# Output products placed between the q projection and the turn of the decayed keys, in a one-core attention and mixture-of-experts kernel

## The reference, cut to what matters

```
xn = _layernorm(x, axis=-1)
q, k, v = silu(xn Wq), silu(xn Wk), silu(xn Wv)           # 16 heads of 32
o = lightning_attn(q, k, v, log_decay)                    # chunks of 128 tokens
gate = (xn Wg1) Wg2
o = o * sigmoid(gate); o = o * rsqrt(mean(o*o over a head) + eps) * norm_w
x = x + o Wo + ffn(xn)                                    # ffn: top 2 of 8 experts, w1, relu, w2
```

## Time and profile before

| what | value |
|---|---|
| median of 3 runs | 2012.76 us (2012.4 to 2012.93) |
| profiled execution | 2013.65 us, of it 2011.9 us span |
| TensorE busy | 1992.8 us, 99% of the span |
| VectorE busy | 892.4 us, 44% |
| ScalarE busy | 552.1 us, 27% |
| GpSimd busy | 721.1 us, 36% |
| mean granted TensorE clock | 0.998 |

### The profile page before, as it was taken

One profiled execution on the slowest core, in us unless ns is written; L12 is line 12 of the kernel. 1 busy time (PEld: TensorE's weight loads), 2 busy tenths in 40 slices (PEclk: granted clock), 3 DMA queues, 4 the chain that ended last, 5 costly groups with the idle time before them and its releaser, 6 DMA issues.

```text
span 2011.9 us, 29144 instructions
## 1 busy us (share of the span) xinstructions
PE 1992.8 (99%) x11768; PEld 1651.0 (82%) x11768; DVE 892.4 (44%) x1792; ACT 552.1 (27%) x986; POOL 721.1 (36%) x600
## 2 busy tenths in 40 slices
PE   8999999999999999999999999999999999999998
PEld 7888888888788888888888888888888888888886
DVE  7777677776742234235323432422252234224311
ACT  6322232223332123124123312421242123123211
POOL 4555553555341323314332331422142324233211
PEclk9999999999999999999999999999999999999999
DMA  6112112211442133315323331521152125224121
GB/s 209 60 64 86 48 61 79 71 66 56 135 135 30 51 79 117 49 48 142 59 63 80 110 50 46 150 50 33 47 160 36 40 47 159 36 62 108 34 33 21
DMA packets 85506, 151.46 MB, mean 75 GB/s; under 512 B 18304, under 2 KB 18304, under 8 KB 85360
## 3 DMA queue, kind: packets, MB, share of 16 engines
q1 hardware_dynamic: 61312, 105.64, 16.4%
q0 software_dynamic: 24048, 43.76, 12.8%
HBM read 109.82 MB, written 39.53 MB: 74 GB/s over the span
## 4 chain that ended last, share of the span: by engine, by line
PE 94%; DMA 2%; issue 1%; DVE 1%; POOL 1%; ACT 0%; POOLq 0%; SPq 0%; DVEq 0%; ACTq 0%
PE bank L1269 47%; PE bank L1562 34%; PE bank L1402 4%; PE bank L1323 2%; PE bank L1617 2%; DMA raw_weights<-in_L_ffn_w 2%; PE bank L1391 1%; PE bank L1276 1%; PE bank L1385 1%; PE bank L1297 1%; PE bank L1358 1%; PE bank L1368 0%; POOL head_scale L588 0%; DMA attn_raw<-in_L_attn_Wv 0%; DMA x_in<-in_L_attn_x 0%
## 5 line engine op out<-in xcount | busy, mean ns | idle before, releaser
L1216 DVE SCALAR_TENSOR_TENSOR h_lo<-bank,h_hi 128x512 fp32r<-128x512 f32 x254 | 175.2, 690 | 745.8 <-ACT h_hi L849 745.6
L632 POOL DMA_INDIRECT gathered<-xn_rows,gather_row x304 | 320.1, 1053 | 476.7 <-DVE x_blocks L1069 294.7
L1269 PE MATMUL bank<-xT_hi,w_hi 128*128 128x512 f32 x1024 | 398.9, 390 | 0.3
L1269 PE MATMUL bank<-xT_lo,w_hi 128*128 128x512 f32 x1024 | 398.5, 389 | 0.0
L1269 PE MATMUL bank<-xT_hi,w_lo 128*128 128x512 f32 x1024 | 398.5, 389 | 0.0
L1562 PE MATMUL bank<-w_hi,h_hi 128*128 128x512 f32 x1016 | 395.5, 389 | 0.7 <-DVE h_lo L1216 0.7
L1562 PE MATMUL bank<-w_hi,h_lo 128*128 128x512 f32 x1016 | 395.3, 389 | 0.0
L1562 PE MATMUL bank<-w_lo,h_hi 128*128 128x512 f32 x1016 | 395.3, 389 | 0.0
L849 ACT ACTIVATE h_hi<-bank 128x512 fp32r<-128x512 f32 x254 | 151.7, 597 | 797.5 <-PE bank L1269 797.5
L645 POOL DMA_INDIRECT out_rows<-y,add_row x80 | 128.8, 1610 | 546.2 <-ACT y L842 473.0
L1269 PEld LDWEIGHTS bank<-xT_hi,w_hi 128*128 128x128 f32 x1024 | 192.2, 188 | 41.7 <-issue 1.7
(11 more groups left out here) (217 smaller groups left out, 2300.1 us busy)
## 6 DMA issues: line engine op xcount, KB each, us to landing
raw_weights<-in_L_ffn_w SPq DMA_DIRECT2D x256, 256.0 KB, 11.7
x_in<-in_L_attn_x SPq DMA_DIRECT2D x32, 256.0 KB, 3.6
xn_rows<-xn SPq DMA_DIRECT2D x32, 256.0 KB, 2.8
x_res<-in_L_attn_x SPq DMA_DIRECT2D x32, 256.0 KB, 5.0
out_rows<-y_attn SPq DMA_DIRECT2D x28, 256.0 KB, 2.0
gathered<-xn_rows,gather_row POOLq DMA_INDIRECT x304
out_rows<-y,add_row POOLq DMA_INDIRECT x80, 5.1
attn_raw<-in_L_attn_Wq SPq DMA_DIRECT2D x4, 256.0 KB, 4.9
```

The lines of the kernel that those rows point to most:

```text
L632: pool.indirect_dma_start(xg[:, nth % 2, q * P:(q + 1) * P], None, xn_pieces, bass.IndirectOffsetOnAxis(ap=gather_row[:, col, q:q + 1], ax ...
L1216: v_.scalar_tensor_tensor(lo[:, 0:n * P], h_bank[f % 2][:, 0:n * P], 0.0, hi[:, 0:n * P].bitcast(F32), ALU.max, ALU.subtract).then_inc(S[" ...
L1269: last = mm(dest, at(left[l], t), at_r(right[r], t), start=(i == 0), stop=(i == n - 1))
```

## The change

Nothing is computed otherwise. In the second slot of groups 1 to 7:

- TensorE makes the four output products behind the q projection, ahead of `turn_kd(u + 1)`, `attend(u)` and `update_states(u + 1)`, and no longer behind these.
- The banks of the output products are swapped: tiles 0 and 2 go to `proj[1]`, tiles 1 and 3 to `proj[0]`. The first waits for `silu_k`, the second for `silu_q`.
- VectorE adds the four residuals (and takes the statistics between them) ahead of `gate_output(u)` and `turn_gated(u)`, which now follow.
- ScalarE makes `oT_hi` ahead of the copy of the turned keys.
- In the third slot the gate's projection waits for all four residuals of the group before, and the k projection no longer waits for a residual.

SP and GpSimd keep their orders.

```diff
@@ ScalarE @@
+                if i == 1 and g > 0:
+                    oT_high(u - 2)
                 if u < ATTN_UNITS - 1:
                     copy_kd(u + 1)
-                if 1 < u < ATTN_UNITS - 1:
+                if 1 < u < ATTN_UNITS - 1 and i != 1:
                     oT_high(u - 2)
@@ VectorE @@
-                gate_output(u)
-                if u != ATTN_UNITS - 2:
-                    turn_gated(u)
+                if i != 1 or g == 0:
+                    gate_output(u)
+                    if u != ATTN_UNITS - 2:
+                        turn_gated(u)
                 if i == 2 and g < SUPERS - 1:
                     oT_low(u - 2)
                 if u == ATTN_UNITS - 3:
                     first_rows()
                 if i == 1 and g > 0:
-                    add_residual(TPG * (g - 1), proj[0])
+                    add_residual(TPG * (g - 1), proj[1])
                     if g < SUPERS - 1:
                         norm_pair(2 * (g + 1) + 1)
-                    add_residual(TPG * (g - 1) + 1, proj[1])
+                    add_residual(TPG * (g - 1) + 1, proj[0])
...
-                    add_residual(TPG * (g - 1) + 2, proj[0])
-                    add_residual(TPG * (g - 1) + 3, proj[1])
+                    add_residual(TPG * (g - 1) + 2, proj[1])
+                    add_residual(TPG * (g - 1) + 3, proj[0])
+                    gate_output(u)
+                    turn_gated(u)
@@ TensorE @@
                 if i == 2:
-                    wait(pe, ("y_ready", TPG * (g - 1) + TPG - 1))
+                    wait(pe, ("y_ready", TPG * g))
...
                 project("q", u + 1, proj[0], "q_projected")
+                if i == 1 and g > 0:
+                    pe.wait_ge(S["attn_w_lo"], WEIGHT_UNITS)
+                    for j in range(TPG):
+                        if j == 0:
+                            pe.wait_ge(S["k_ready"], u + 2)
+                            wait(pe, ("oT_lo_made", TPG * g - 1))
+                        elif j == 1:
+                            pe.wait_ge(S["q_ready"], u + 2)
+                        else:
+                            wait(pe, ("y_ready", TPG * (g - 1) + j - 1))
+                        project_out(j, proj[1 - j % 2], range(GROUPS), True, True, GROUPS * g if j == 0 else None)
```

More of the change, by code:

```diff
@@ L1469, in _ @@
                 pe.wait_ge(S["k_ready"], u + 1)
-                if i == 2:
-                    wait(pe, ("y_ready", TPG * g))
                 project("k", u + 1, proj[1], "k_projected")
@@ L1484, in _ @@
                     update_states(u + 1)
-                if i == 1 and g > 0:
-                    pe.wait_ge(S["attn_w_lo"], WEIGHT_UNITS)
-                    for j in range(TPG):
-                        if j == 0:
-                            pe.wait_ge(S["q_ready"], u + 2)
-                            wait(pe, ("oT_lo_made", TPG * g - 1))
-                        elif j == 1:
-                            pe.wait_ge(S["k_ready"], u + 2)
-                        else:
-                            wait(pe, ("y_ready", TPG * (g - 1) + j - 1))
-                        project_out(j, proj[j % 2], range(GROUPS), True, True, GROUPS * g if j == 0 else None)
                 if i == GROUPS - 1:
```

## The result

The changed kernel takes 2018.16 us (median of 13 runs, 2017.15 to 2019.57), the kernel before, run beside it, 2013.17 (13 runs, 2012.32 to 2015.79). The ratio is 1.0024, with a 95% interval of 1.0016 to 1.0032: 5.0 us slower, where the forecast was 6.2 us and 2019.0. The profiled execution of after has a span of 2016.7 us at a granted clock of 0.998, 4.8 us more than before's 2011.9.

What follows compares the result with a forecast made beforehand. TensorE, busy 99% of the span, was taken as the bound. Middle groups 2.2, last group 2.4, gathers 0.8 and clock 0.8 sum to 6.2 us, giving 2019.0 us, 0.3% slower; range 2015.5 to 2022.0.

Steps and rivals of the forecast that it cites:

- Bound and pace: TensorE, busy 99% of the span, sets the time; one output product takes 0.227 us, a change to small matmuls 0.23.
- Switches saved: Output products behind the q projection need no change between kinds of matmul: 0.2 us less in each of 7 groups.
- First wait: Middle groups: the tenth output matmul waits for oT_lo, 0.4 us in even groups, 0 to 0.1 in odd ones.
- Second wait: Middle groups: rstd behind qdT delays normed tiles and masks, so the normed tokens' turn waits: 0.4 us even, 0.3 odd.
- Rival 1: Middle groups cost nothing, only the last group does: 2014.8 us, within 0.2%; chance 0.13.
- rival 2: Lateness grows: xnT_lo holds the fourth slot, each middle group pays another 0.7 us, 2023.2 us, slower; chance 0.11.
- Rival 4: Faster, through hidden waits ahead of the turn of keys; switches alone give 1.4 us, 2011.4; chance 0.03.
- Last group: Second slot: third output product idles 3.1 us for a residual behind the slot records; next scores 2.4 us later.
- list of signs that it is wrong: Slot records landing earlier against the q projection's end, scores starting at 505.8 there, or idle time elsewhere, such as the fourth slot.
- Rival 3: Not slower: records back before 497.0, 2.2 us earlier, so no wait in the last group: 2015.6 us; chance 0.07.
- Gathers: Last unit's turn of keys waits for kdT, behind four GpSimd gathers queued after the delayed qdT: 0.8 us.
- The clock: TensorE's idle time in the last group may drop its clock to 1.2 GHz: 0 or 1.7 us, middle 0.8.

Runs made afterwards that it cites:

- e9: Changed kernel with e5's two edits, rstd ahead of qdT, normed tiles ahead of gated output, mean square behind normed in second slots: 2012.76 us, ratio 0.9997.
- e4: Changed kernel with rstd made ahead of qdT on GpSimd in the second slots of groups 1 to 6: 2016.77 us, ratio 1.0017 to the kernel before.
- e3: Changed kernel with VectorE's first_row moved behind all four residuals of the last group: 2015.50 us, ratio 1.0014 to the kernel before.
- e5: Changed kernel with first_row behind the last group's second residual and split weights, and GpSimd's four gathers ahead of qdT: 2014.66 us, ratio 1.0008.
- e6: Changed kernel with the first three fourths of output tiles 0 and 1 ahead of both tiles' last fourths: 2019.60 us, ratio 1.0031.
- e2: Kernel before with the change made in the last group only: 2016.51 us, ratio 1.0015.
- e10: Changed kernel with an unread VectorE product and transposition added between oT_lo and first_row of the last group: 2019.79 us, ratio 1.0030.
- e1: Kernel before with the change made in groups 1 to 6 only: 2015.52 us, ratio 1.0013.
- e7: Changed kernel with e5's edits, rstd ahead of qdT, normed tiles ahead of the gated output, and e6's order of products: 2013.94 us, ratio 1.0004.
- e11: Kernel before with 150 already met waits put into TensorE's program ahead of the last group's second-slot projections: 2051.22 us (one run), beside 2035.92 for before.
- e12: As e11, but in the kernel before with the last group's second-slot gated output and its turn behind the residuals: 2051.68 us (one run).

## Why the prediction was right, and where it was not

**Bound and pace.** As said: no engine has more work, and TensorE's stops make the difference.

**Switches saved.** The step's 0.2 us a group was too much. In odd groups, where the first wait was to cost 0 to 0.1 and 0.2 to be saved, after gained 0.06; e9, with nearly all waits gone, gains 0.06 in an odd group too.

**First wait, `oT_lo`.** Right in place and cause. An even group costs 0.25 to 0.28 us to the third slot's scores (forecast 0.4 - 0.2 = 0.2), with a stop of 0.3 at the tenth product; e4 leaves just this. The net fits because two sizes are off together: less saved by the switches and less paid for the wait.

**Second wait, `rstd` behind `qdT`.** Right in place, cause and size: 0.28 to 0.31 us a group (forecast 0.4 and 0.3), and e4 takes it away with one swap on GpSimd. An even group came to 0.55 to 0.59 us and an odd one to 0.22, forecast 0.6 and 0.15; the sum is 2.34 for 2.2. Rival 1, margins that vanish, and rival 2, a lateness that grows, both fell: the fourth slot shows no wait. Rival 4 had only the switches to live on.

**Last group, 2.4 us.** The mechanism was right, as e3 shows; the size was not: 1.55. The step that failed is "the records come back at 499.22: nothing that makes them is moved". Nothing was moved, but the scatter's completion is no constant: from its start to the load it took 3.15 us before and 2.17 after. 7.62 - 6.76 = 0.86 us is the whole of what the term was off. Records that land earlier against the q projection's end are on the prediction's own list of signs that it is wrong, and for this term they were. What stood in the step's place is a packet of the program's loading beside the scatter in before, whose end a landing signal followed by 1.26 us. The change moved nothing of SP's or GpSimd's, but it moved TensorE's instructions, and with them the packets: beside the scatter there is none in after nor in any kernel that has the products of the last group in the new place. Rival 3 asked for more than it says: the third product starts 500.14 - 499.22 = 0.92 us behind the records, so they would have had to be back at 497.05 - 0.92 = 496.1, 3.1 us earlier and not 2.2. They came 0.86 earlier.

**Gathers, 0.8 us.** Right: 0.79, and 0.00 in e5. GpSimd's timeline of after has the last gather (the first starts at 512.23) and the last unit's `kdT` behind it, as forecast:

```profile
516.28 1.00 POOL L596 DMA_INDIRECT y<-xn_rows,first_row  x1 [0.30 <-issue]
517.30 1.01 POOL L537 TENSOR_TENSOR kdT<-kT,k_decay 128x384 f32<-128x384 f32 x1
```

**The clock, 0.8 us as the middle of 0 and 1.7.** It is one or the other: of five profiles with the stop (1.88 to 2.15 us) after, e4 and e6 kept 1.00, e2 and e10 paid 1.62 and 1.63 us. After's own profile paid nothing. The Trainium skill (TensorE: Matmul & The Clock Gate, section "Why this matters for your kernels") warns of idle gaps longer than these stops came out. Two of the five profiles lost the clock all the same, so here the measurement goes further than the page.

**The sum.** In the profile 2.34 + 1.55 + 0.79 + 0 = 4.68 us. The profile's span grew by 4.9 before rounding: the shift of 1.0 at the start and the 0.8 won back in the experts belong to no term, and that they nearly cancel is luck. The medians differ by 5.0, which agrees with 4.68 and a part of the clock's price in some runs; that share wasn't measured. The forecast of 6.2 is 1.5 above the profile's sum: 0.85 in the last group's term and 0.8 for the clock, less 0.14 in the middle groups.

## What to carry to other kernels

Where an engine has no idle time, a move can only pay for what it hides, and everything queued behind the moved work on the other engines must be followed: here an `rstd` of 0.69 us behind a multiplication that now waits, and a single small read of slot records ahead of four residuals, cost 1.7 us (e4) and 2.2 us (e3), and swaps of order brought both back. A wait repaired at one place of a ring of buffers comes back at the next (e6); ask what the ring's other end waits for before adding work ahead of a completion. A duration from a row of a transfer holds only as long as what runs beside it stays, even for a transfer that nobody touches, and the loading of the program is one of the things beside it, which moves when instructions move. A term that rests on such a row deserves the range of the same transfer in other places: before's own scatters would have shown both landing times.

## What of the hardware was not expected

**The same stop, two clocks.** An idle time of 1.91 us on TensorE is followed by the 1.2 GHz level in e2 and stays without it in after, with the same instructions around it. The same is seen at the start, where TensorE waits for the first logits: 2.83 us in before, followed by a stretch at half clock, 3.83 in after, with the same, and 3.15 in e1, with the clock at 1.00 throughout. By the second unit's scores, in kernels whose instructions are alike to that point, the shifts of the table's column "start" are there, -0.1 to +2.3 us. The clock alone doesn't make them: e2 and e7 kept it there and stand within 0.1 us of before, which lost it, and after is late already when TensorE starts again, at 27.17 for 26.15. A single profile can't tell a change of 1 to 2 us in this kernel; the starts of later units against each other can.

**A small indirect scatter takes 2.17 us or up to 3.15** from start to the load that waits for it, with nothing changed about it. One of its 16 landing signals comes about 1.1 us behind the end of a 16 KB packet of the program's loading, where such a packet runs beside it, and the next scatter's 0.17 us later. The filler of e10 also stretched the last scatter's own time on GpSimd, the only run to show it:

```profile
497.82 1.13 POOL L580 DMA_INDIRECT slot_table<-record,slot_no  x1 [0.30 <-issue]
```

It is 0.97 us for that scatter in the others. The Trainium skill (GPSIMD Engine Reference, section "Specifications") says that GpSimd shares its memory interfaces with VectorE, and that a VectorE instruction with two operands in SBUF gets in its way; the filler's has two, the gated output of before has one there and one in a bank. The 0.16 us agree with that, but the filler's transposition lay beside the scatter too, and no run parts the two.

**A wait that is met still costs the sequencer.** The 150 instructions that the waits of e11 became cost 10.6 us of TensorE's time, more than the work queued ahead of them could cover, and the granted clock stood at 0.50 behind both stops.

**The same kernel, 2013 or 2036 us.** Beside e11 and e12 the kernel before took 2035.92 us (one run), 22.8 more than the median measured beside after. Its granted clock was 0.998 then too, and the chip's number is the same as for e1 to e4, where it took 2012.94 an hour before; whether it was the same chip isn't known, so that chips differ isn't shown. TensorE's waits of e11 between 90 and 480 us have rows that no other profile but e12's has:

```profile
PEld bank L1368 <- issue: 14.2, 27, 0.6
PE bank L1368 <- issue: 11.2, 23, 1.2
```

In the stretches of small matmuls (the updates of the states) it stood for about 0.47 us at a time, waiting for nothing that the profile shows. The 11.2 us are half of the 22.2 by which unit 28 came later than in before's profile; a slower supply of instructions would look like this, but no run here tests it.
